# A recommendation tower on one core: row gathers that also wait for the portion of products that is running

## What is computed

```python
e = stack([tbl_f[ids[:, f]] for f in range(32)], axis=1)     # 2048 x 32 x 256, float32
z = einsum('bnd,bmd->bnm', e, e)[:, iu, ju]                  # 496 pairs i < j of the 32 fields
h = concatenate([z, dense_ctx], axis=1)                      # 2048 x 512
h = maximum(h @ W_top1 + b_top1, 0)                          # 512 x 512
h = maximum(h @ W_top2 + b_top2, 0)                          # 512 x 256
y = h @ W_top3                                               # 2048 x 1
```

## Time and profile before

| what | value |
|---|---|
| runs: median (lowest to highest of 3) | 564.66 us (564.0 to 564.92) |
| traced execution: its span, the one time that is known of it | 890.7 us |
| TensorE matmul busy in it | 601.0 us, 67% |
| POOL busy in it | 398.0 us, 45% |
| mean granted TensorE clock in it | 0.850 |
| gathers | 419 of 128 KB |

### The profile page before, as it was taken

How to read it: one execution, slowest core, us unless ns; L and a number is a source line. 1 busy time by engine, 2 the same in 40 slices (tenths; PEclk the granted TensorE clock), 3 DMA queues, 4 the chain that set the end, 5 groups by cost and what they waited for, 6 DMA issues and landing times.

```text
span 890.7 us, 24184 instructions
## 1 busy us (share of the span) xinstructions
PE 601.0 (67%) x11019; PEld 524.1 (59%) x11019; DVE 225.9 (25%) x578; ACT 204.6 (23%) x369; POOL 398.0 (45%) x426
## 2 busy tenths in 40 slices
PE   3557668486684867748577584875848668486687
PEld 2456557375572756737467474765737657375586
DVE  3444313123130231402223032231312313123122
ACT  4252303103030030401313022130210303103042
POOL 7563625526255361543715347262462625526220
PEclk9688969698796987969789697896969969698799
DMA  9962312313122141321313224131231312313110
GB/s 220 243 204 68 99 42 77 94 44 102 43 78 83 50 107 38 83 73 56 108 37 87 63 57 118 32 96 49 70 105 39 101 41 76 88 41 90 43 38 2
DMA packets 37459, 70.97 MB, mean 80 GB/s; under 512 B 10382, under 2 KB 23438, under 8 KB 37358
## 3 DMA queue, kind: packets, MB, share of 16 engines
q0 software_dynamic: 20112, 54.95, 22.1%
q1 hardware_dynamic: 17246, 14.48, 7.0%
HBM read 69.39 MB, written 0.01 MB: 78 GB/s over the span
## 4 chain that ended last, share of the span: by engine, by line
PE 42%; another core or an unknown queue 30%; issue 13%; ACT 12%; DMA 1%; DVE 1%; POOL 1%; ACTq 0%; DVEq 0%
PE look_ps L338 18%; PE quad_ps L358 12%; PE top_ps L420 6%; ACT turned L501 4%; ACT turned L483 3%; PE turn_ps L322 3%; PE quad_ps L322 2%; ACT area L550 2%; ACT ahead L490 1%; DMA rows<-in_tbl,row_ids 1%; PE quad_ps L377 1%; POOL rows L295 1%; PE top_ps L407 1%; ACT products L506 0%
## 5 line engine op out<-in xcount | busy, mean ns | idle before, releaser
L295 POOL DMA_INDIRECT rows<-in_tbl,row_ids x419 | 397.2, 948 | 458.1 <-PE turn_ps L322 184.1
L338 PE MATMUL look_ps<-one_hot,small 125*128 125x256 f32 (+1 forms) x1536 | 251.9, 303 | 104.7 <-issue 92.8
L338 PEld LDWEIGHTS look_ps<-one_hot,small 125*128 125x128 f32 x1536 | 214.0, 202 | 116.6 <-issue 112.3
L358 PE MATMUL quad_ps<-turned 128*32 128x31 f32 x7680 | 140.0, 204 | 121.8 <-issue 121.5
L358 PEld LDWEIGHTS quad_ps<-turned 128*32 128x32 f32 x7680 | 108.8, 115 | 166.9 <-issue 153.3
L674 DVE TENSOR_SCALAR one_hot<-ids_across,sub_row 125x256 fp32r<-125x256 int32 (+1 forms) x384 | 112.0, 364 | 145.8 <-PE look_ps L338 126.6
L322 PE MATMUL turn_ps<-ident,rows 128*128 128x128 f32 x424 | 64.5, 282 | 28.5 <-issue 14.7
L655 DVE TENSOR_TENSOR top_ps<-top_ps,b_sb 128x256 f32<-128x256 f32 x15 | 6.5, 433 | 299.8 <-PE top_ps L420 299.8
L490 ACT ACTIVATE ahead<-look_ps 128x512 f32<-128x512 f32 (+1 forms) x48 | 28.3, 590 | 232.5 <-PE look_ps L338 219.1
L407 PE MATMUL top_ps<-area,w_sb 128*128 128x128 f32 x488 | 61.9, 276 | 19.5 <-issue 18.8
L550 ACT ACTIVATE area<-top_ps,b_sb 128x128 f32<-128x128 f32 x61 | 17.5, 368 | 227.5 <-remote 225.2
(11 more groups left out here) (50 smaller groups left out, 169.9 us busy)
## 6 DMA issues: line engine op xcount, KB each, us to landing
rows<-in_tbl,row_ids POOLq DMA_INDIRECT x419
ids_across<-in_small_ids SPq DMA_DIRECT2D x45, 128.0 KB
landed<-in_tbl SPq DMA_DIRECT2D x6, 896.0 KB
w_sb<-in_W_top SPq DMA_DIRECT2D x4, 256.0 KB
landed<-in_tbl SPq DMA_DIRECT2D x6, 104.0 KB
w_sb<-in_W_top SPq DMA_DIRECT2D x1, 512.0 KB
area<-in_dense_ctx SPq DMA_DIRECT2D x16, 8.0 KB
row_ids<-in_ids SPq DMA_DIRECT2D x1, 240.0 KB
```

The costliest lines, as they stand in the source:

```text
L295: pool.indirect_dma_start(out=rows[:, n % PLACES, j, :], out_offset=None, in_=tables[f], in_offset=bass.IndirectOffsetOnAxis(ap=row_ids[:, ...
L338: last = pe.matmul(look_ps[:, c * width:(c + 1) * width], small[:, f, r, part, c * P:(c + 1) * P], one_hot[n % 2][:, r, 0:width], start=(r ...
L358: last = pe.matmul(gram_ps[q * FIELDS:(q + 1) * FIELDS, g // BANK_GROUPS, at:at + COLS], turned[:, c, s, :], turned[:, c, s, 0:COLS], star ...
```

## The change

A table says, for each of a tile's units by its number in the tile, in which portion of the tile ahead its gather may begin. Units 0 to 2 have no entry; units 3 to 12 wait for the begin of portions 0, 1, 2, 2, 3, 4, 5, 6, 6 and 7 of the gram of tile t-1. A portion counts as begun when the first product of its first group is done, on TensorE. The wait for a free place stays. Tile 0 has no such waits, and the last tile's own gram signals nothing, since no tile follows. The order of the instructions on each engine stays as it was, and so do their numbers; the line numbers move by up to seven.

```diff
+    GATHER_IN = [None, None, None, 0, 1, 2, 2, 3, 4, 5, 6, 6, 7]
...
+        portion_begun = sem("portion_begun")
...
                 if n >= PLACES:
                     pool.wait_ge(turn_done, n - PLACES + 1)
+                if t > 0 and GATHER_IN[n - BEGIN[t]] is not None:
+                    pool.wait_ge(portion_begun, (t - 1) * PARTS + GATHER_IN[n - BEGIN[t]] + 1)
                 for j, f in enumerate(unit):
                     pool.indirect_dma_start(
...
                                              start=(c == 0), stop=(c == CHUNKS - 1))
+                            if g == portion * GPP and c == 0 and q == 0:
+                                last.then_inc(portion_begun, 1)
```

## The result

The change makes the kernel slower: median 609.21 us (607.25 to 616.18, 4 runs) against 564.33 us (563.0 to 564.92, 4 runs) for the kernel before, ratio 1.083 with a 95% interval of 1.076 to 1.090. The direction was forecast, the size was not: 45 us instead of 24.5.

A forecast was written before the change was run, and what follows sets the result against it. POOL, issuing gathers at 1.25 us each, was taken as the bound: 564.66 + 19.6 (waits in fourteen tiles) + 4.9 (first gated tile) = 589.2 us. The forecast's own range was 571 to 603, with rivals 556 to 608.

The forecast's parts named there:

- In the runs POOL issues gathers almost without a break: All tiles before the change: POOL needs 32.5 us a tile, TensorE 30.9, so TensorE waits for each tile's last units.
- the 9 us left for idle time: Kernel before: 555.5 us with POOL never idle against runs of 564.66 us; the remainder, placed ahead of tile 2.
- Entries 2 to 7 free: Waits of units 5 to 12 for portions 2 to 7: never the last to be met, cost nothing.
- L - 0.1 us in each tile: POOL's idle time at unit 4's wait for portion 1, paid in every tile: 14 x 1.4 = 19.6 us.
- L: Landing: from the end of unit 12's last gather row to TensorE's turn of that unit, taken as 1.5 us.
- The first gated tile, 4.9 us: Tile 2's first gather starts 25.5 instead of 20.6 us behind tile 0's first product, as tile 1's gathers wait.
- Rival C, the clock: TensorE's longer wait in each tile brings clock 0.50: 1.4 us in each of 14 tiles, 20 more, 609; chance 0.06.
- such a clock stands behind some seventeen disturbed microseconds, not three: Argument against rival C: clock 0.50 follows long disturbed stretches, not TensorE's wait of 3.0 us a tile.
- the loop: Portion 1's gate delays later gathers through unit 12, which TensorE needs next; tiles 1 to 14, 19.6 us.

The follow-up runs named there:

- the second trace: The kernel before the change, unaltered, executed once more for its trace: 562.7 us.
- experiment 2: Kernel before, in tiles 1 to 15 without the second field's gather of unit 12: 545.5 us; of units 3, 6, 9 and 12: 542.6 us.
- experiment 4: Changed kernel with only the waits of units 3 and 4: 605.7 us; with those two taken out and the other eight kept: 610.7 us.
- experiments 8 and 1: 8: changed kernel, tile 1's gathers free of the new waits, 599.0 us. 1: changed kernel, table empty, signals kept, 562.6 us.
- experiment 6: Changed kernel plus added matmuls on TensorE while it waits for units 11 and 12 in tiles 2 to 15: 595.8 us, ratio 1.058 to the kernel before.

## Why the prediction was right and wrong

- **"In the runs POOL issues gathers almost without a break"**: right, shown by the second trace and by experiment 2. The argument stood on a trace that was no picture of the runs; what held was the pace of a row, 1.25 us, and the sum against the runs. Of the 9 us left for idle time, 2 are the difference between the median and the execution traced (562.71), 1.8 lie outside its span, 2 are a longer end (30.8 us behind the end of the last gather, where 28.8 were counted), and some 3 are idle time.
- **Entries 2 to 7 free**: right while the first two stand (experiment 4). Without those, portion 2's entry takes their place. The gathers wait mostly at units 3 and 4 and keep their pace, as forecast; that TensorE's pauses would move into all portions was wrong, since there were none.
- **"L - 0.1 us in each tile", 1.4 us**: the mechanism was right, the term too small. In tile 8 of the change, at full clock, it is 1.85. L is 1.85 there and 1.79 to 1.95 in all fourteen tiles, not 1.5. From portion 1's first row to the gather that it frees, 1.02 us pass, not 0.47. The layers and lookups between are 0.46 us quicker than taken (9.30 us from unit 12's turn to portion 1, not 9.76). Fourteen tiles make 26 us instead of 19.6.
- **The first gated tile, 4.9 us**: 8.29 us of idle time beyond the usual at unit 3 of tile 1, against 2.5 us at unit 9 of tile 1 and unit 0 of tile 2 in the undisturbed trace before: 5.8. Right in kind and nearly in size, though not sharply: the traces of experiments 8 and 1, also without gates there, have 3.4 and 5.5 us in these two places.
- **Rival C, the clock, "such a clock stands behind some seventeen disturbed microseconds, not three"**: this step failed. With it the sum put the clock at nothing, and C got 6%. The rows didn't say so even then. The seventeen are the whole stretch; TensorE's first pause in it ends at 432.16 after 0.78 us, and in the stretch from 436 to 437 the clock is already at 0.56 (stretches of the trace of the kernel before, columns as in rows 4):

```profile
435.00:436.00 1.00, 0.31 (x2) 0.49 (x3) 0.00 (x0) 0.00 (x0) 0.86 (x1) 1.00 0.71 213
436.00:437.00 1.00, 0.46 (x2) 0.00 (x0) 0.00 (x0) 0.00 (x0) 0.83 (x1) 0.56 0.43 131
437.00:438.00 1.00, 0.21 (x2) 0.49 (x3) 0.00 (x0) 0.00 (x0) 0.70 (x2) 0.50 0.27 74
```

In the changed kernel it fell behind less than that: ahead of six of fourteen tiles it was at 0.50, behind waits for units 11 and 12 that together were 2.7 to 3.7 us. What is left of the 43.7 us after 26 and 5.8 is 12 us, 1.4 to 2.9 in each of the six tiles; 10.3 of it is the longer layer 1, and about one is the unexplained wait in tile 4. Experiment 6 took 13.4 us away, 2.8 of them behind the last gather. That the time is C's own figure, 609, is luck: C had 1.4 us in each of fourteen tiles, 20 in all; the runs have 12 in six tiles, and the rest comes from the larger loop, tile 1 and the end. The Trainium skill's page "TensorE: Matmul & The Clock Gate", Part 1, cited there, says that idleness brings the half-rate clock back. The traces agree: 0.50 behind the waits, 3.74 us of layer 1 where experiment 6 filled them. That the longer wait is the likelier to bring it shows only roughly: the eight tiles that stayed at full clock had 2.6 to 3.0 us.

Forecast and measured then differ by 6 (the loop), 1 (tile 1), 12 (the tiles behind a slow layer 1) and 1 (the end): 20 of the 45 us.

## What to carry to other kernels

When the engine that issues transfers is the bound, every new wait on it must be laid against the moment it would have come to that place anyway: a gate that opens 1.5 us late in a loop is paid in each turn, and the same table set a portion earlier cost 8 us instead of 45. A traced span that is far from the timed runs is to be traced again before any of its waits is mended; here the pauses that spreading the gathers could have cured were not in the runs. And a wait that lands on TensorE can cost a second time, when the clock falls behind it and the slower work lies in the loop: that price belongs into the sum, not into a rival beside it.

## What was not expected of the hardware

A signal set on the first product of a portion reaches GpSimd late: in tile 8 of the change, and in tile 8 of experiment 4, the gather starts 1.02 to 1.03 us behind the portion's first row (303.06 to 304.09, 307.01 to 308.03, 310.12 to 311.15). That is 0.31 us behind the start of what follows the portion (303.78), so "has begun" came there no sooner than the portion's end. It isn't the end that opens the gate, though. In experiment 4's trace portion 2 of tile 0 breaks off after nine products, and the gather starts while the other 55 run:

```profile
59.87 0.28 PE L363 MATMUL quad_ps<-turned 128*32 128x31 f32 x9
...
60.70 0.68 PE L363 MATMUL quad_ps<-turned 128*32 128x31 f32 x55 [0.55 <-issue]
...
60.89 0.95 POOL L300 DMA_INDIRECT rows<-in_tbl,row_ids  x1 [9.51 <-PE quad_ps L363]
```

Again it starts 1.02 us behind the first row, and 0.49 us ahead of the portion's end. So the distance goes with the first product; what it consists of, no run shows.

The clock didn't fall behind every wait: 2.54 and 0.50 us brought 0.50 in one tile, 2.44 and 0.53 us left it at 1.00 in the one before.
